# Causal attention with 16 heads of width 8: value products for eight heads at a time, two heads to 32 array columns, and a new layout of all jobs of a batch

## The chip, the cores and the metric

One core of one Trainium2 chip runs the kernel. The metric is the device time of one execution in microseconds (us); lower is better.

## The reference, cut to what matters

```python
xn = layernorm(x)                               # x: (8, 512, 128) f32
q, k, v = split(xn @ w_attn.T + b_attn)         # 16 heads of width 8
att = (q @ k.T) / sqrt(8), causal
S  = relu(att of head 0), column 0 and the diagonal set to 0
FF = cumsum over the queries of S shifted down by one row
att = att - FF                                  # for every head
keep = the 101 smallest FF of a row (fewer in the first rows), and the diagonal
y = softmax(where(keep, att, -inf)) @ v
attn = y @ w_proj.T + b_proj
# router: top 2 of 8 experts per token
ffn = sum over e of gate_e * (relu(xn @ wi.T + bi + (xn @ A_e.T) @ B_e.T) @ wo.T + bo)
out = x + attn + ffn
```

## The kernel before, in words

Eight batches are worked through one after the other. A batch's attention is cut into 44 units: for a tile `a` of 128 queries (four of them) a unit is four heads (`a` = 0), two heads (`a` = 1) or one head (`a` = 2, 3), against the `a + 1` key tiles up to the diagonal (`UNITS`, L59). Units are numbered through over all batches, and every engine runs the same loop over steps `t`, from -26 to the end, each in its own program and held together by semaphores. In step `t`

- PE makes the scores of unit `t` (`score`, L895) into one of three banks `ps_s`, turns unit `t - 4` by transposes into one of two banks `ps_t` (`turn`, L914), fills the jobs that the plan puts into this step (`fill`, L749), and, where unit `t - 5` ends a group of four heads, makes the value products of the group (`weigh`, L927): one f32 product for every head and key tile, which the trace shows as two instructions. The stationary operand is 32 columns of `va` (8 of v, one of ones for the sum of the weights, and what comes next), the moving one 128 columns of the exponentials `pr`. Four heads stand beside one another in the 128 array columns, and write 32 partitions each of `ps_o`.
- DVE adds the mask and takes the maximum of each row (L1320, L1327 for tile 0, L1330 for the others); POOL subtracts it (L549, `ar`); ACT takes the exponential out of `ps_t` into one of six buffers `pr` (L734). ACT waits with it until the products that read the buffer before are done.

When all groups of a query tile are done, ACT copies `ps_o` to `out_t` (L743, `taken`); the next tile's first group waits for that. The job `ot` (L869) turns the copy back by four transposes, DVE divides by the sums (L1292, L1294), the job `yt` (L875) transposes the result, ACT copies it, and the job `proj` projects three tiles (`proj0`) and then the last (`proj1`), with DVE adding the rest and SP storing `res` (L368).

A job is a piece of PE work with a step, one of two banks `ps_m` and a reader (ACT or DVE). `class Plan` (L134) sorts the jobs by step; a job waits for the read of the one that had its bank before, two jobs ago. The steps are written out by hand: `FFN_JOBS`, `OT_AT`, `YT_AT`, `PROJ_AT` count from a batch's own first unit, `PREP_AT` counts from the first unit of the batch before, since a batch is prepared while the one before it is worked on; `FIRST_AT` and `SECOND_AT` do so for the first two. Preparing is: layernorm (`moments`, `root`, `norm`, `xt`), q and k, each cut into three bf16 parts (`rest`, `second`, `third`), their head-stacks `qs`, `ks`, v (`v0`, `v1`: one copy each of v for two key tiles, one of the router's logits), head 0's scores (`s0` to `s3`, L812, read by ACT, L696), the sums over the queries (`forget`, L1085, `scan0` to `scan3`), their transposes (`f0` to `f3`), a search for the cut that keeps 101 keys (`search`, `under`, `reach`, `marks`, `top`, `replace`), a check (`flag`) and the masks (`mask_0` to `mask_3`, POOL, L536). The feed-forward part has `z`, two router masks (`mask0`, `mask1`), eight `h` jobs and two `down` jobs; ACT reads the `h`, POOL adds two of them to `hsum` (L563).

SP issues all transfers in one order (L432): the stacks of the next batch (`make_stacks`, 12 transfers of 128 KB), the second store of the batch before, the fetch of an input, the first store of this batch, and `make_first_heads` for the batch after the next (L400: 12 transfers of 8 KB, six for q and six for k). `s0` waits for these (`topped`, L820).

## Time and profile before

| | |
|---|---|
| median of 3 runs | 660.26 us (660.19 to 662.8) |
| the profiled execution | 663.88 us, its span 661.9 us |
| busy over the span | PE 561.8, DVE 505.3, POOL 445.7, ACT 378.0 us |
| mean granted TensorE clock | 0.958 |

Times are us unless marked ns. PEld is PE's weight load, which overlaps its products. "Idle before", in brackets at the end of a timeline row, is how long the engine had nothing to do before it, and what ended that. A busy PE is not a PE at its peak, since each instruction is shown with the tail in which the next one already runs: the step from one start to the next tells what it costs. Where a row says "x32", 32 instructions of a line are merged.

### The profile page before, as it was taken

How to read it: one execution, taken by the hardware profiler on the slowest of the kernel's cores; microseconds unless marked ns; L12 is line 12 of the kernel's file. 1: busy time of each engine (PE TensorE's matmuls, PEld its weight loads, DVE VectorE, ACT ScalarE, POOL GpSimd, SP SyncE). 2: the span in 40 equal slices, each digit the busy share in tenths (PEclk: the TensorE clock that was granted, in tenths of full speed). 3: DMA queues.
4: the chain of work that ended last, by engine and by line, in shares of the span. 5: the costliest groups of instructions: out<-in, count | busy, mean ns of one | idle time of the engine just before them, and what ended most of it. 6: DMA issues, size and time to landing. Idle time of an engine off the chain costs nothing.

```text
span 661.9 us, 16486 instructions
## 1 busy us (share of the span) xinstructions
PE 561.8 (85%) x5434; PEld 382.5 (58%) x5434; DVE 505.3 (76%) x1832; ACT 378.0 (57%) x815; POOL 445.7 (67%) x756
## 2 busy tenths in 40 slices
PE   4636879989888899889998898989998899899994
PEld 1413555766466665656566565666566565776583
DVE  7679798667997679857897769867897769975351
ACT  3452776565765565754756566664756556455542
POOL 7506948696578746796478955798478956496451
PEclk9656999999999899989999999999999999999998
DMA  4152052134001520025100430025000430000000
GB/s 100 25 63 27 1 63 35 30 47 61 1 17 28 65 30 1 18 47 63 11 18 17 60 45 1 17 43 70 9 1 18 60 44 1 2 14 5 1 2 17
DMA packets 30068, 19.56 MB, mean 30 GB/s; under 512 B 6089, under 2 KB 29856, under 8 KB 29984
## 3 DMA queue, kind: packets, MB, share of 16 engines
q1 hardware_dynamic: 29984, 18.50, 19.5%
q8 instruction: 45, 0.74, 0.5%
q14 instruction: 39, 0.32, 0.2%
HBM read 3.22 MB, written 2.10 MB: 8 GB/s over the span
## 4 chain that ended last, share of the span: by engine, by line
PE 41%; DVE 19%; POOL 15%; issue 11%; ACT 7%; SPq 4%; DMA 1%; DVEq 1%; ACTq 0%; POOLq 0%
PE ps_t L923 10%; POOL ar L549 9%; PE ps_o L942 9%; PE ps_s L910 6%; PE ps_m L855 4%; SPq L407 4%; DVE ar L1330 4%; ACT work L648 2%; PE ps_m L851 2%; DVE work L1150 2%; PE ps_m L867 2%; ACT pr L734 2%; POOL hsum L563 1%; PE ps_m L873 1%; PE ps_m L885 1%
## 5 line engine op out<-in xcount | busy, mean ns | idle before, releaser
L549 POOL TENSOR_SCALAR ar<-ar,mx 128x512 f32<-128x512 f32 (+3 forms) x512 | 280.2, 561 | 171.4 <-DVE mx L1330 165.1
L734 ACT ACTIVATE pr<-ps_t 128x512 f32<-128x512 f32 (+1 forms) x352 | 192.4, 558 | 80.9 <-PE ps_t L923 78.8
L1330 DVE CUSTOM_DVE_ANT_0 ar<-ps_s,mask 128x256 f32<-128x256 f32 (+2 forms) x384 | 202.9, 550 | 33.2 <-PE ps_s L910 32.3
L923 PE MATMUL ps_t<-ident,ar 128*128 128x128 f32 x1280 | 202.6, 277 | 16.5 <-POOL ar L549 11.0
L923 PEld LDWEIGHTS ps_t<-ident,ar 128*128 128x128 f32 x1280 | 156.2, 142 | 57.2 <-POOL ar L549 27.4
L910 PE MATMUL ps_s<-ks,qs 96*128 96x512 bf16 (+3 forms) x512 | 130.4, 307 | 11.7 <-DVE mx L1327 6.0
L942 PE MATMUL ps_o<-pr,va 128*32 128x128 f32 x2560 | 98.8, 282 | 7.6 <-ACT pr L734 6.1
L942 PEld LDWEIGHTS ps_o<-pr,va 128*32 128x32 f32 x2560 | 63.4, 111 | 48.5 <-ACT pr L734 31.2
L910 PEld LDWEIGHTS ps_s<-ks,qs 96*128 96x128 bf16 x512 | 43.1, 99 | 56.5 <-issue 27.1
L719 ACT ACTIVATE h<-ps_m,bi_col 128x512 f32<-128x512 f32 x64 | 43.9, 687 | 54.9 <-PE ps_m L855 54.2
L855 PE MATMUL ps_m<-zm,b_t 128*128 128x512 f32 x128 | 67.7, 610 | 8.7 <-ACT h L719 8.7
L563 POOL TENSOR_TENSOR hsum<-h 128x512 f32<-128x512 f32 x32 | 42.5, 1329 | 0.0
L648 ACT ACTIVATE work<-nf,cut 128x384 f32<-128x384 f32 (+1 forms) x48 | 31.7, 666 | 15.5 <-DVE cut L1128 10.8
L855 PEld LDWEIGHTS ps_m<-zm,b_t 128*128 128x128 f32 x128 | 21.7, 189 | 30.1 <-issue 15.3
L1091 DVE TENSOR_TENSOR_SCAN ft<-ones,s 128x511 f32<-128x511 f32 (+3 forms) x32 | 30.4, 959 | 6.2 <-POOL s L520 5.7
L851 PE MATMUL ps_m<-xnt,wi_t 128*128 128x512 f32 x64 | 33.5, 605 | 1.2 <-ACT h L719 1.2
L696 ACT ACTIVATE s<-ps_m,not_first 128x128 f32<-128x128 f32 (+3 forms) x29 | 15.2, 522 | 31.7 <-PE ps_m L821 27.3
L1189 DVE MAX8 top<-work 128x8 f32<-128x400 f32 (+3 forms) x64 | 30.9, 504 | 1.9
L1330 DVE DVE_READ_ACCUMULATOR2_ANT mx<- 128x1 f32 x384 | 31.4, 82 | 0.0
L1197 DVE MATCH_REPLACE8 work<-top,work 128x400 f32<-128x400 f32 (+3 forms) x64 | 31.3, 492 | 0.0
L867 PE MATMUL ps_m<-wo_t,hsum 128*128 128x128 f32 x256 | 31.2, 275 | 0.0
L867 PEld LDWEIGHTS ps_m<-wo_t,hsum 128*128 128x128 f32 x256 | 29.8, 192 | 0.1
(227 smaller groups left out, 772.1 us busy)
## 6 DMA issues: line engine op xcount, KB each, us to landing
qs<-parts SPq DMA_DIRECT2D x42, 128.0 KB
ks<-parts SPq DMA_DIRECT2D x42, 128.0 KB
xs<-in_L_attn_x SPq DMA_DIRECT2D x8, 256.0 KB, 3.0
out<-res SPq DMA_DIRECT2D x8, 192.0 KB, 2.0
first_heads<-parts SPq DMA_DIRECT2D x72, 8.0 KB
qs<-parts SPq DMA_DIRECT2D x12, 64.0 KB
ks<-parts SPq DMA_DIRECT2D x12, 64.0 KB
out<-res SPq DMA_DIRECT2D x8, 64.0 KB, 10.5
```

Source lines behind the costliest of these rows:

```text
L549: nc.gpsimd.tensor_scalar(col, col, -1.0, mx[:, t % NA_RING, j:j + 1], ALU.mult, ALU.add)\
L563: nc.gpsimd.tensor_tensor(hsum[:, f, :], h[:, 2 * (f % 2), :], h[:, 2 * (f % 2) + 1, :], ALU.add).then_inc(h_sum, 1)
L648: nc.scalar.activation(work[:, a, PADS:PADS + P * (a + 1)], nf[:, OFF[a]:OFF[a + 1]], ACT.Sign, bias=cut[:, a:a + 1], scale=-float(2 ** (R ...
L719: nc.scalar.activation(h[:, 2 * (f % 2) + j, :], m[:, :], ACT.Relu, bias=bi_col[:, f:f + 1])\
L734: nc.scalar.activation(pr[:, u % NP_RING, 0:w], ps_t[u % NT_RING][:, 0:w], ACT.Exp, scale=-1.0)\
L851: nc.tensor.matmul(m[:, :], wi_t[:, P * f:P * f + P], xnt[:, n % 2, :], start=True, stop=False)
L855: last = nc.tensor.matmul(m[:, :], b_t[:, P * f:P * f + P], zm[:, j, :], start=False, stop=True, skip_group_check=(j == 1))
L867: last = nc.tensor.matmul(m[:, P * a:P * a + P], hsum[:, f, P * a:P * a + P], wo_t[:, f, :], start=False, stop=(a == hi - 1 and f == NF - 1))
L910: last = nc.tensor.matmul(ps_s[u % NS_RING][:, w * j:w * j + w], qs[:, k % 2, h0 + j, P * a:P * a + P], ks[:, k % 2, h0 + j, 0:w], start=T ...
L923: last = nc.tensor.transpose(ps_t[u % NT_RING][:, P * j:P * j + P], ar[:, u % NA_RING, P * j:P * j + P], ident[:, :])
L942: last = nc.tensor.matmul(ps_o[OW * j:OW * j + OW, P * group:P * group + P], va[:, k % 2, c, VW * hh:VW * hh + OW], pr[:, (NU * k + unit) ...
L1330: nc.vector.tensor_tensor_reduce(out=ar[:, t % NA_RING, w * j:w * j + w], in0=ps_s[t % NS_RING][:, w * j:w * j + w], in1=mask[:, k % 2, OF ...
```

## The change

- `weigh` runs for eight heads (`OCT`): head pairs share 32 array columns. `va` holds a pair in 41 columns: 9 of the one head, 9 zeros from column 16, 9 of the other head from column 32. The stationary window of 32 columns starts at column 0 for the one head and at 16 for the other, so that each adds zeros to the other's 9 partitions, and both are summed into the same 32 partitions. `ORDER` names the heads so that the eight come out in order.
- A query tile takes 256 columns of `ps_o`, and two tiles share the bank: `taken`, `ot` and `yt` run twice in a batch, and the projections take two tiles each.
- `pr` has 11 buffers. Room for them comes from buffers that others lie in now: `s0` in `work`, `ft` in `hsum`, `qk32` in `h`, `ones` is a quarter as wide. New waits keep them apart.
- v is copied in four pieces per job. `first_heads` takes six transfers with q and k in one, and SP makes them ahead of the first store.
- The steps of all jobs are set anew.

```diff
-OW = 512 // NH
+OW = 32
+HALF_OW = OW // 2
+PAIR = 41
+OUT_COLS = HALF_OW * NH
...
-NA_RING, NP_RING = 7, 6
+NA_RING, NP_RING = 7, 11
...
-QUAD = 4
-GROUPS = NH // QUAD
-GROUP_OF = [GROUPS * a + h // QUAD for a, h, g in UNITS]
+QUAD, OCT = 4, 8
+GROUPS = NH // OCT
+GROUP_OF = [GROUPS * a + h // OCT for a, h, g in UNITS]
+
+ORDER = [8 * (i // 8) + 2 * (i % 4) + i % 8 // 4 for i in range(NH)]
...
-FIRST_FFN = ffn_jobs(6, (17, 19), (22, 24, 27, 30), (34, 36))
-FFN_JOBS = ffn_jobs(4, (8, 8), (15, 18, 21, 23), (29, 31))
-OT_AT, YT_AT, PROJ_AT = (12, 19, 36, 50), (17, 22, 39, 52), (40, 55)
-ATT_JOBS = [(f"ot{a}", OT_AT[a], "dve") for a in range(NA)] + [(f"yt{a}", YT_AT[a], "act") for a in range(NA)] + \
+FIRST_FFN = ffn_jobs(3, (17, 18), (19, 22, 24, 26), (40, 42))
+FFN_JOBS = ffn_jobs(4, (6, 10), (16, 18, 22, 24), (29, 30))
+OT_AT, YT_AT, PROJ_AT = (20, 52), (21, 53), (45, 54)
+ATT_JOBS = [(f"ot{a}", OT_AT[a], "dve") for a in range(2)] + [(f"yt{a}", YT_AT[a], "act") for a in range(2)] + \
...
-    "flag": 24, "mask_0": 24, "mask_1": 24, "v0": 21, "v1": 26, "marks_middle": 26, "top0_middle": 26,
-    "replace0_middle": 27, "top1_middle": 27, "replace1_middle": 28, "marks_wide": 25, "top0_wide": 25,
-    "replace0_wide": 26, "top1_wide": 26, "replace1_wide": 27, "last": 29, "mask_2": 30, "mask_3": 32,
-    "route": 30, "choices": 37, "share": 38,
+    "flag": 24, "mask_0": 24, "mask_1": 24, "v0": 10, "v1": 17, "marks_middle": 26, "top0_middle": 26,
+    "replace0_middle": 27, "top1_middle": 29, "replace1_middle": 30, "marks_wide": 25, "top0_wide": 25,
+    "replace0_wide": 26, "top1_wide": 28, "replace1_wide": 29, "last": 31, "mask_2": 32, "mask_3": 32,
+    "route": 26, "choices": 38, "share": 39,
...
-    "moments": -23, "root": -23, "norm": -5, "xt": -4, "q": 9, "k": 10, "rest_q": 10, "second_q": 11,
-    "third_q": 12, "rest_k": 11, "second_k": 12, "third_k": 12,
+    "moments": -23, "root": -23, "norm": -5, "xt": -4, "q": 9, "k": 12, "rest_q": 10, "second_q": 11,
+    "third_q": 12, "rest_k": 13, "second_k": 14, "third_k": 15,
...
-    "moments": -22, "root": -17, "norm": -15, "xt": -12, "q": -11, "k": -10, "rest_q": -10, "second_q": -9,
-    "third_q": -8, "rest_k": -9, "second_k": -8, "third_k": -7, "v0": 11, "v1": 13, "route": 14, "choices": 22,
-    "share": 23, "s0": 3, "s1": 5, "s2": 7, "s3": 9, "scan0": 6, "scan1": 6, "scan2": 10, "scan3": 12, "f0": 9,
-    "f1": 12, "f2": 13, "f3": 15, "search": 16, "under": 22, "reach": 23, "marks_narrow": 24,
-    "marks_middle": 26, "marks_wide": 27, "top0_narrow": 24, "top0_middle": 26, "top0_wide": 29,
-    "replace0_narrow": 27, "replace0_middle": 28, "replace0_wide": 30, "top1_narrow": 34, "top1_middle": 31,
-    "top1_wide": 35, "replace1_narrow": 35, "replace1_middle": 31, "replace1_wide": 35, "flag": 37,
-    "mask_0": 38, "mask_1": 38, "mask_2": 41, "mask_3": 45,
+    "moments": -30, "root": -17, "norm": -15, "xt": -12, "q": -11, "k": -10, "rest_q": -10, "second_q": -9,
+    "third_q": -8, "rest_k": -9, "second_k": -8, "third_k": -7, "v0": 15, "v1": 15, "route": 15, "choices": 21,
+    "share": 31, "s0": 3, "s1": 5, "s2": 7, "s3": 9, "scan0": 6, "scan1": 9, "scan2": 10, "scan3": 12,
+    "f0": 11, "f1": 11, "f2": 14, "f3": 14, "search": 15, "under": 21, "reach": 23, "marks_narrow": 28,
+    "marks_middle": 24, "marks_wide": 26, "top0_narrow": 28, "top0_middle": 25, "top0_wide": 27,
+    "replace0_narrow": 28, "replace0_middle": 26, "replace0_wide": 29, "top1_narrow": 31, "top1_middle": 36,
+    "top1_wide": 29, "replace1_narrow": 35, "replace1_middle": 36, "replace1_wide": 37, "flag": 38,
+    "mask_0": 40, "mask_1": 40, "mask_2": 44, "mask_3": 47,
 }
 PREP_JOBS = [("xt", "act"), ("q", "act"), ("k", "act"), ("v0", "act"), ("v1", "act")] + \
...
-        bias_rows = sb("bias_rows", [ROWS, 2, NA - 1, C], BF16)
+        bias_rows = sb("bias_rows", [ROWS, 2, 2, C], BF16)
...
-        va = sb("va", [P, 2, NA, (NH - 1) * VW + OW])
-        s0 = sb("s0", [P, FOFF[NA]])
-        ft = sb("ft", [P, FOFF[NA]])
+        va = sb("va", [P, 2, NA, NH // 2 * PAIR + VW])
         nf = sb("nf", [P, OFF[NA]])
         work = sb("work", [P, NA, WIDE])
+
+        s0_place = ((0, 1), (1, 1), (2, 1), (1, 3 * P + 2))
+
+        def s0(j, lo, hi):
+            row, at = s0_place[j]
+            return work[:, row, at + lo:at + hi]
...
+        qk32 = h
...
+        ft = hsum[:, :, :].rearrange("p f t -> p (f t)")
...
                         wait_full(sp, "s3", m - 1)
-                        for t in range(2):
-                            sp.wait_ge(split, 2 * m + t + 1)
-                            part = (Q_PART, K_PART)[t]
-                            for j in range(len(part)):
-                                sp.dma_start(first_heads[8 * j:8 * j + 8, t, :], parts[0:P:NH, t, part[j], :])\
-                                    .then_inc(topped, 16)
+                        sp.wait_ge(split, 2 * m + 2)
+                        for j in range(len(Q_PART)):
+                            lo, hi = Q_PART[j], 3 + K_PART[j]
+                            sp.dma_start(first_heads[8 * j:8 * j + 8, :, :],
+                                         parts[0:P:NH, :, :, :].rearrange("p t j c -> p (t j) c")[:, lo:hi + 1:hi - lo, :])\
+                                .then_inc(topped, 16)
...
                             fetch(k + 3)
-                        store(sp, k, 0)
                         if k + 2 < B:
                             make_first_heads(k + 2)
+                        store(sp, k, 0)
...
+                    link(nc.gpsimd.memset(work[:, 0:3, 0:1], 0.0))
+                    link(nc.gpsimd.memset(work[:, 1, 3 * P + 1:3 * P + 2], 0.0))
                     link(nc.gpsimd.memset(va[:, :, :, :], 1.0))
+                    for p in range(NH // 2):
+                        link(nc.gpsimd.memset(va[:, :, :, PAIR * p + HALF_OW:PAIR * p + HALF_OW + VW], 0.0))
...
                                     if f == 0:
+                                        if k + 1 < B:
+                                            wait_full(pool, f"f{NA - 1}", k + 1)
...
+                                    if n >= 2:
+                                        act.wait_ge(h_sum, NF * (n - 1))
...
-                                    act.wait_ge(scanned, NA * (n - 1) + j + 1)
+                                    act.wait_ge(mask_done, NA * (n - 1) + s0_place[j][0] + 1)
...
-                                copy(va[:, into(n), both, 0:NH * VW].rearrange("p a (h d) -> p a h d", d=VW)[:, :, :, 0:HD],
-                                     m3[:, :, 0:P].rearrange("p a (h d) -> p a h d", d=HD), name, n, False)
+                                for i, a in enumerate(half):
+                                    for s in range(2):
+                                        copy(va[:, into(n), a, 0:NH // 2 * PAIR]
+                                             .rearrange("p (h d) -> p h d", d=PAIR)[:, :, OW * s:OW * s + HD],
+                                             m3[:, i, 0:P].rearrange("p (h s d) -> p h s d", s=2, d=HD)[:, :, s, :],
+                                             name, n, False)
...
                                 f, j = int(name[1]), int(name[2])
+                                act.wait_ge(rested, 2 * min(n + 2, B))
...
-                            for a in range(NA):
+                            for a in (1, 3):
                                 if t == NU * kk + LAST[a] + LAG_P + OUT_LAG:
...
-                            last = nc.tensor.transpose(m[:, 0:P], y[:, a, :, :].rearrange("p h d -> p (h d)"), ident[:, :])
+                            for i in range(2):
+                                last = nc.tensor.transpose(m[:, P * i:P * i + P],
+                                                           y[:, 2 * a + i, :, :].rearrange("p h d -> p (h d)"), ident[:, :])
...
-                        if group == 0 and NA * k + a >= 1:
-                            pe.wait_ge(taken, NA * k + a)
-                        elif group == 0:
+                        if group == 0 and a % 2 == 0 and 2 * k + a // 2 >= 1:
+                            pe.wait_ge(taken, 2 * k + a // 2)
+                        elif group == 0 and a == 0:
...
+                        col = OUT_COLS * (a % 2) + P * group
                         for c in range(a + 1):
-                            for j in range(QUAD):
-                                hh = QUAD * group + j
+                            for j in range(OCT):
+                                hh = OCT * group + j
+                                quarter, odd = j % QUAD, j // QUAD
                                 unit, at = PLACE_OF[a, hh]
                                 at = P * (at + c)
-                                last = nc.tensor.matmul(ps_o[OW * j:OW * j + OW, P * group:P * group + P],
-                                                        va[:, k % 2, c, VW * hh:VW * hh + OW],
+                                from_v = PAIR * (ORDER[hh] // 2) + HALF_OW * odd
+                                last = nc.tensor.matmul(ps_o[OW * quarter:OW * quarter + OW, col:col + P],
+                                                        va[:, k % 2, c, from_v:from_v + OW],
                                                         pr[:, (NU * k + unit) % NP_RING, at:at + P],
-                                                        start=(c == 0), stop=(c == a))
+                                                        start=(c == 0 and odd == 0), stop=(c == a and odd == 1))
...
-                            link(nc.vector.memset(ft[:, FOFF[a]:FOFF[a] + 1], 0.0))
...
-                        for a in range(1, NA - 1):
+                        for a in range(1, 2):
                             link(nc.vector.tensor_copy(bias_part[:, :, :, a, :], bias_part[:, :, :, 0, :]))
...
-                        if j == 0 and n >= 1:
-                            wait_full(dve, f"f{NA - 1}", n - 1)
+                        if j == 0 and n == 1:
+                            wait_full(dve, f"f{NA - 1}", 0)
+                            dve.wait_ge(w_rows, 32)
+                        elif j == 0 and n >= 2:
+                            wait_full(dve, "down1", n - 2)
...
-                                    y[:, a, :, :], o3[:, :, 0:HD],
-                                    rec[:, :].rearrange("p (h o) -> p h o", o=1).to_broadcast([P, NH, HD]), ALU.mult)\
+                                    y[:, 2 * a:2 * a + 2, :, :].rearrange("p a h d -> p (a h) d"), o4[:, :, 0:HD],
+                                    rec[:, :].rearrange("p (g o) -> p g o", o=1).to_broadcast([P, 2 * NH, HD]), ALU.mult)\
```

## Rows read from the trace of the kernel before

**Rows 1.** the chain that ended last: shares by engine, by line

```profile
PE 41%; DVE 19%; POOL 15%; issue 11%; ACT 7%; SPq 4%; DMA 1%; DVEq 1%; ACTq 0%; POOLq 0%
PE ps_t L923 10%; POOL ar L549 9%; PE ps_o L942 9%; PE ps_s L910 6%; PE ps_m L855 4%; SPq L407 4%; DVE ar L1330 4%; ACT work L648 2%; PE ps_m L851 2%; DVE work L1150 2%; PE ps_m L867 2%; ACT pr L734 2%; POOL hsum L563 1%; PE ps_m L873 1%; PE ps_m L885 1%
```

**Rows 2.** windows by batch: length, then PE, PEld, DVE, ACT, POOL, clock

```profile
65.00:140.60 75.60, 64.90 (x620) 43.82 (x620) 61.93 (x224) 48.29 (x104) 56.39 (x88) 0.99 0.22 31
140.60:215.40 74.80, 66.54 (x675) 45.94 (x674) 60.78 (x227) 45.96 (x101) 55.38 (x93) 1.00 0.21 32
215.40:292.50 77.10, 68.34 (x675) 47.42 (x674) 61.61 (x225) 46.14 (x101) 53.33 (x93) 0.97 0.22 30
292.50:367.00 74.50, 67.03 (x668) 45.66 (x668) 59.06 (x221) 45.12 (x98) 52.44 (x90) 0.98 0.22 29
367.00:441.00 74.00, 66.62 (x674) 45.80 (x672) 60.10 (x224) 45.94 (x99) 53.92 (x91) 1.00 0.21 31
441.00:517.00 76.00, 67.56 (x682) 46.87 (x683) 62.32 (x228) 46.57 (x101) 56.51 (x98) 1.00 0.20 29
...
590.00:662.00 72.00, 61.23 (x660) 42.48 (x658) 31.87 (x117) 33.04 (x63) 36.82 (x62) 0.97 0.02 6
```

**Rows 3.** timeline of PE, two product calls and a job: start, length

```profile
370.59 0.43 PE L942 MATMUL ps_o<-pr,va 128*32 128x128 f32 x8
370.95 0.39 PE L910 MATMUL ps_s<-ks,qs 96*128 96x256 bf16 x2
...
426.04 0.60 PE L873 MATMUL ps_m<-ident,out_t 128*128 128x128 f32 x4
426.57 1.08 PE L942 MATMUL ps_o<-pr,va 128*32 128x128 f32 x32
427.58 0.39 PE L910 MATMUL ps_s<-ks,qs 96*128 96x512 bf16 x1
```

**Rows 4.** copies on ACT by line: count, ns shortest/median/longest, starts, forms

```profile
L743 ACT ACTIVATE out_t<-ps_o x32: 591/599/607, 70.0 to 653.2; 128x512 f32<-128x512 f32 x32
...
L575 ACT ACTIVATE yt<-ps_m x32: 255/274/289, 87.5 to 655.7; 128x128 f32<-128x128 f32 x32
L575 ACT ACTIVATE va<-ps_m x15: 363/387/392, 50.2 to 534.9; 128x256 f32<-128x256 f32 x15
L575 ACT ACTIVATE no_bias<-ps_m x15: 172/177/178, 50.5 to 535.2; 128x16 f32<-128x16 f32 x15
```

**Rows 5.** timeline of SP; then PE's waits: total, times, longest

```profile
433.13 7.31 SPq L407 DMA_DIRECT2D first_heads<-parts  x12
440.54 3.92 SPq L397 DMA_DIRECT2D qs<-parts  x6
...
PE ps_m L821 <- DMA first_heads<-parts: 10.4, 6, 2.1
...
PE ps_m L821 <- DVE zm L1277: 5.4, 6, 1.2
```

**Rows 6.** timeline of PE, longest wait for first_heads; a window behind it

```profile
291.21 0.38 PE L821 MATMUL ps_m<-first_heads 96*128 96x512 bf16 x1 [2.10 <-DMA first_heads<-parts]
...
294.10 1.64 PE L942 MATMUL ps_o<-pr,va 128*32 128x128 f32 x32
...
292.00:294.00 2.00, 2.00 (x5) 0.59 (x3) 0.62 (x4) 0.80 (x2) 2.00 (x5) 0.50 0.58 79
```

**Rows 7.** timeline of DVE, two scores, last batch; its waits for scores

```profile
641.02 0.69 DVE L1330 CUSTOM_DVE_ANT_0 ar<-ps_s,mask 128x512 f32<-128x512 f32 x1
...
641.67 0.69 DVE L1330 CUSTOM_DVE_ANT_0 ar<-ps_s,mask 128x512 f32<-128x512 f32 x1
...
DVE ar L1330 <- PE ps_s L910: 32.3, 37, 3.5
```

**Rows 8.** timeline of POOL at the start

```profile
4.52 1.22 POOL L477 MEMSET va<- 128x1336 f32 x1
...
18.89 0.23 POOL L493 TENSOR_SCALAR minus_mean<-mv 128x4 f32<-128x4 f32 x1 [3.55 <-DVE mv L1016]
```

More of the change, by code:

```diff
@@ L194, in build @@
         ident16 = sb("ident16", [P, P], BF16)
-        ones = sb("ones", [P, T])
+        ones = sb("ones", [P, P])
         causal = sb("causal", [P, P])
@@ L722, in _ @@
                                 a = int(name[2])
-                                if n >= 1 and a in (0, 3):
-                                    wait_full(act, ("proj0", "proj1")[a == 3], n - 1)
-                                copy(yt[:, a, :], m[:, 0:P], name, n)
+                                if n >= 1:
+                                    wait_full(act, f"proj{a}", n - 1)
+                                copy(yt[:, 2 * a:2 * a + 2, :].rearrange("p a t -> p (a t)"), m[:, 0:2 * P], name, n)
                         u = t - LAG_T
@@ L870, in fill @@
                             a = int(name[2])
-                            pe.wait_ge(taken, NA * n + a + 1)
-                            for c in range(GROUPS):
+                            pe.wait_ge(taken, 2 * n + a + 1)
+                            for c in range(4):
                                 last = nc.tensor.transpose(m[:, P * c:P * c + P], out_t[:, P * c:P * c + P],
```

51 lines of the change are left out of this document (25 added, 26 removed).

## The prediction

> **What bounds the kernel now.** The chain that ended last comes first: TensorE (PE) holds 41% of it, VectorE (DVE) 19%, GpSimd (POOL) 15%, the SP queue 4%, waits that the profile can't name 11% [rows 1]. No engine holds it alone: by line the turning of the scores, POOL's shift and the value products stand close together. The stretches from one batch's router product to the next come second [rows 2]: six inner batches take 74.0 to 77.1 us, with PE busy for 65 to 68 of them, DVE for 59 to 62, POOL for 52 to 57, ScalarE (ACT) for 45 to 48. The last batch, with DVE busy for 31.87 us only, still takes 72 us. The reader is to see there that taking half of DVE's work away saved hardly 3%: PE's queue, with its waits, sets the pace through most of a batch, and the others set it only at the edges. Third is PE's own order of time inside a batch [rows 3], for the price of one call, and fourth the waits ahead of PE [rows 5].
>
> **Value products.** Work stays: per batch 320 product instructions before and after, with the same 128 columns. What goes is calls, 16 per batch before, 8 after. From the start of a call to the start of the next score is 0.36 us for 8 instructions and 1.01 for 32 [rows 3]: 27 ns each and about 0.14 us per call. Ahead of the call comes another gap. The four transposes show 0.60 us there, 0.16 of it the last one's tail as the call's own 1.08 us has one, and 0.53 lie between their start and the call's, so some 0.09. I take 0.24 us a call with both. 64 calls fewer give 15.4 us of PE time. How much of it is path? The line has 9% of the chain, 60 us [rows 1], of 2560 x 27 ns plus 128 x 0.24 us, 100 us: 0.6. Taken: **-9.2 us**. Bounds: 0 and -15.4.
>
> **Output tiles.** Two query tiles of 256 columns fill the bank that one filled, so 32 copies of it on ACT become 16, and 32 jobs of four transposes become 16. A job costs PE 0.53 us with its gap [rows 3]; 16 x 0.53 is 8.5 us. Its line has 1% of the chain, 6.6 us of 17, so 0.39. Taken: **-3.3 us**, bounds 0 and -8.5. ACT loses 16 x 0.60 us of copies and 16 of 32 small yt copies, which become wider ones [rows 4]; that is off the path, since ACT is busy 45 to 48 us of a batch. If that cover goes, it is a gain of some 10 us more on ACT alone. DVE has 16 reciprocals and 16 products fewer, of twice the width; I cost them at nothing, under the same waits.
>
> **The v copies.** One copy of 0.387 us per v job becomes four of a quarter of the width. The rows bound one of 128x64 between 0.177 us (128x16) and 0.274 us (128x128) [rows 4], nearer to the lower end in columns: 0.21. So ACT gets 4 x 0.21 - 0.39, 0.45 us more per job, and both v jobs now lie in one step (15, before 11 and 13). With the two bias-free copies that is a block of 2.0 us on ACT (1.8 to 2.5), and queued behind it are the exponentials that the next turn needs for its bank. Two banks give PE one step of some 1 us. Taken: 0.4 us a batch, **+3 us**, bounds 0 and +10.
>
> **The first heads.** PE waited six times for these transfers, 10.4 us, 2.10 at most [rows 5, 6]. SP issues 12 of them behind the store of the first projection, in 7.31 us [rows 5]. Now 6 wider ones stand ahead of the store, whose own wait (proj0, step 40, now 45) no longer holds them. What they wait for instead is the third part of k at step 37, just before. An issue costs 0.61 us in this row, next to the 0.65 us of one with 128 KB in the row under it; twice the bytes should not double it. So 3.7 to 3.9 us of issue in place of 7.31 (7.3 at the worst), and a start up to a few us earlier: the longest wait, 2.10, is covered. Behind them in SP's queue the store and then the next batch's 12 stack transfers move later; the stacks aren't needed for a whole batch, and the store's buffer not before the next proj0. Stretches that ended with such a wait on the chain took 75.6, 74.8, 77.1 and 76.0 us, the other two 74.5 and 74.0 [rows 2]: 1.6 us apart, four times. Taken: **-6.5 us**, bounds -1 and -10.4 plus what the clock gives (below).
> After the 2.10 us wait PE's granted clock is 0.50, its lower level of 1.2 GHz, in the next 2 us and a product call of 32 takes 1.64 us [rows 6], against 1.08 [rows 3]. Part of the 1.6 us is this. The Trainium skill, "TensorE: Matmul & The Clock Gate", the section on the HAM clock gate, says that the throttled state is the default and that activity releases it. By that rule a shorter gap gives more than its own length, and by the same rule a new gap costs more than its own.
>
> **Router masks.** Both mask products lay in step 8 and their readers on DVE ran back to back; PE waited 5.4 us for them at the s job alone [rows 5]. Now they are in steps 6 and 10, with one scan moved from 6 to 9. Taken: **-3 us**, bounds 0 and -5.4.
>
> **Aliases.** The head-0 scores, the forgetting sums and q, k lie in buffers of other steps now. Each brings a wait: s on masks of 7 steps before, the first sum of h on f3 (14, against 17), the sums on down1, far back, q on the sums of h (25, against 33). All have slack of two steps or more, so nothing. A late f3 would be paid by POOL's sum and then by ACT's h.
>
> **The rest.** At the start, POOL fills a va of twice the size (+1.22 us) and ten small pieces more, about 3 us in all; a little later it sits idle for 3.55 us [rows 8], and DVE saves 1 to 2 us of small sets and copies. Taken 0, bounds -2 and +3. At the end, the last call has 64 instructions instead of 32 (+0.88 us) and six operations on two tiles; twice the width costs 0.11 us (0.274 to 0.387 [rows 4]), so +0.7; the call four steps before, 1.0 us [rows 3], is gone, and I count half of it. Taken **+1.1 us**.
>
> Sum: -9.2 - 3.3 + 3 - 6.5 - 3 + 0 + 1.1 = -17.9 us. Against the profiled execution's 663.9 us (span 661.9) that is 646.0; it ran 3.6 us over the median, so against 660.26 it is 642.4. **Forecast 642 us**, itself 634 to 652 for the spread of the terms.
>
> **Rivals.**
> *PE's work comes off in full* (chance 0.12). For it speaks the last batch, 72 us with DVE at 31.87. Then -15.4 - 8.5 - 10.4 - 3 + 2 is -35: 625 us.
> *PE is not what the time hangs on.* (0.19) DVE's and POOL's chain takes over, 59 to 62 and 52 to 57 us busy in a batch [rows 2] and in step with each other, and PE's freed time turns into waits for them. Only the transfers and half of the tiles' work come off, and the v block costs its 3: -6.5 - 1.6 + 3 + 1.1, about -4 to -8: 654 us. The inner 74.0 us stretch, which has no late transfer, speaks for it.
> *Long calls starve the scores* (0.12), the case on the other side. A call of 64 instructions holds PE for 32 x 27 ns more than one of 32: 1.9 us, plus the next score's 0.22. DVE eats one 512-column score in 0.65 us (two follow at that distance [rows 7]), and there are three score banks, so 1.95 us of supply. From a supply below 2.1 us on, and always where a long job of the feed-forward part lies beside it, DVE and behind it POOL run dry. Each batch has two such calls in each of tiles 1, 2 and 3, 0.43, 0.65 and 0.86 us longer: 3.9 us a batch, 31 in all. If half shows, 15.5, and the call's gain of 9.2 is lost, 642 becomes 667 us. Against it: DVE and POOL have 12 to 20 us of slack in a batch to catch up.
> *The new layout opens a gap in PE at each batch and the clock falls there* (0.07). Two us at 0.50 lose 1.0 us and the call behind them 0.56 [rows 6], with a gap of 2 us itself 3.6; seven times is 25, so 667 us. This is the rule named above from the Trainium skill, "TensorE: Matmul & The Clock Gate", used against the change. Against it: idle time moves from PE only where PE was the later one.
> *The change doesn't do what it says*: the product count is plain in the code, so no chance of its own.
>
> **Numbers.** The forecast's case has 0.50, and with the rivals' 0.12, 0.19, 0.12 and 0.07 that is all. The least that a measurement of this kernel can tell from no change is about 0.5%, 3.3 us, so faster is below 657 us. Faster: 0.48 of the forecast's case, the full one, and 0.14 of the second, 0.74. Within it: 0.02 of the first, 0.05 of the second and 0.01 of the starved one, 0.08. Slower: 0.11 of the starved and the clock's 0.07, 0.18. The range takes in the full case's centre and the second rival and stops at the mild end of the slower ones, 625 to 663 us, which leaves out some 0.15 above and 0.05 below.
>
> **What would show it.** Right: 64 product calls and 16 output jobs; PE busy per inner batch down by 2 to 3 us with the stretch down by about as much (72 us); no wait for first_heads, SP's six issues under 6 us; granted clock 1.00 in the stretches that show 0.97 now. Wrong: DVE idle for the scores after long calls, up from 32.3 us in all [rows 7]; ACT's block at step 15 followed by a PE wait for pr; batches still at 74 us with the same PE gaps for POOL; or new waits of PE over 2 us with the clock at 0.50 behind them.

## The result, and the profile after

The changed kernel takes **632.10 us** (median of four, 630.34 to 633.98), the kernel before beside it 660.23 (658.28 to 662.8). The ratio is 0.9573, with a 95% interval from 0.9527 to 0.9618: faster by 4.3%. The profiled execution took 633.0 us with a span of 631.2, so it is 0.9 over its median, where that of before was 3.6 over. The forecast was 642; 632.1 lies in its range (625 to 663), 2 us below the forecast case's own (634 to 652).

The profile's page of the changed kernel, busy time, then the chain that ended last by engine and by line (lines moved: L549 of before is L566, L910 L938, L923 L951, L942 L973, L1330 L1362):

```profile
PE 538.6 (85%) x5370; PEld 377.6 (60%) x5370; DVE 500.2 (79%) x1795; ACT 371.1 (59%) x831; POOL 447.5 (71%) x766
...
PE 35%; DVE 24%; POOL 23%; issue 9%; ACT 6%; SPq 1%; DVEq 0%; DMA 0%; ACTq 0%; POOLq 0%
POOL ar L566 14%; PE ps_t L951 8%; PE ps_m L881 7%; DVE ar L1362 6%; PE ps_o L973 6%; PE ps_s L938 4%; POOL mask L553 4%; PE ps_m L877 3%; DVE work L1229 3%; POOL zm L525 2%; DVE top L1221 2%; ACT work L667 2%; POOL parts L530 2%; ACT pr L760 1%; ACT h L745 1%
```

PE fell from 41% of the chain to 35, the SP queue from 4 to 1, the products' line from 9 to 6; POOL rose from 15% to 23 [rows 1]. The time came off PE and off a transfer, and the chain of DVE and POOL now holds more of what is left.

The same, windows by batch, each from the first score of a batch that DVE reads to the next batch's (columns as in [rows 2]):

```profile
133.45:204.12 70.67, 64.10 (x660) 45.47 (x659) 60.11 (x222) 44.16 (x101) 53.00 (x91) 0.98 0.24 38
204.12:274.04 69.92, 63.46 (x668) 45.45 (x667) 60.75 (x221) 45.28 (x102) 54.32 (x93) 1.00 0.24 33
...
416.76:486.55 69.79, 63.41 (x668) 45.39 (x667) 60.65 (x220) 45.12 (x102) 54.25 (x93) 1.00 0.23 29
...
554.28:631.20 76.92, 63.35 (x724) 46.13 (x722) 36.56 (x121) 35.63 (x66) 43.64 (x77) 0.97 0.03 9
```

The kernel before, cut at the same point, in a batch with the full clock:

```profile
436.43:510.65 74.22, 66.53 (x676) 45.93 (x675) 60.64 (x225) 45.95 (x100) 54.82 (x93) 1.00 0.20 28
```

An inner batch went from 74.2 us to 69.8: 4.4 off, of which PE's busy time is 3.1 and its waits the rest, while DVE and POOL have the same work. By this cut the batches of before take 83.2, 74.2, 76.9, 76.2, 74.9, 74.2, 74.2 and 77.1 us, those of after 82.0, 70.7, 69.9, 72.8, 69.9, 69.8, 67.7 and 76.9. The first and the last gave 1.4 together. Of the second to the sixth batch of a kernel, those at full clock and without such a single wait as named below are alike within some 1 us, mostly within 0.1. They are called clean in what follows, and 74.2 and 69.8 us are clean ones. The 72.8 us batch holds one wait of 2.7 us for which the profile names nothing.

PE's timeline in the changed kernel: a call of eight heads, its neighbours, and the output job (start, length):

```profile
422.56 1.95 PE L973 MATMUL ps_o<-pr,va 128*32 128x128 f32 x64
424.45 0.39 PE L938 MATMUL ps_s<-ks,qs 96*128 96x256 bf16 x2
...
430.27 0.60 PE L899 MATMUL ps_m<-ident,out_t 128*128 128x128 f32 x4
430.80 0.65 PE L973 MATMUL ps_o<-pr,va 128*32 128x128 f32 x16
```

64 instructions take 1.89 us from start to start: 64 x 27 ns + 0.14, as read off [rows 3]. What DVE does meanwhile is in its timeline, with the waits for scores behind the two calls of 64 and the two of 48 in this batch (starts 422.56, 459.39, 471.65, 482.18):

```profile
424.88 0.42 DVE L1362 CUSTOM_DVE_ANT_0 ar<-ps_s,mask 128x256 f32<-128x256 f32 x1 [0.54 <-PE ps_s L938]
462.57 0.56 DVE L1362 CUSTOM_DVE_ANT_0 ar<-ps_s,mask 128x384 f32<-128x384 f32 x1 [0.20 <-PE ps_s L938]
475.05 0.69 DVE L1362 CUSTOM_DVE_ANT_0 ar<-ps_s,mask 128x512 f32<-128x512 f32 x1 [0.33 <-PE ps_s L938]
484.50 0.69 DVE L1362 CUSTOM_DVE_ANT_0 ar<-ps_s,mask 128x512 f32<-128x512 f32 x1 [0.59 <-PE ps_s L938]
```

DVE waits 0.2 to 0.6 us behind each of these calls; how much of that is due to their length, e4 tells. The waits, in all (total, times, longest), and SP's order of work around 413 to 430:

```profile
POOL ar L566 <- DVE mx L1362: 132.2, 121, 3.5
DVE ar L1362 <- PE ps_s L938: 39.7, 46, 4.0
PE ps_t L951 <- POOL ar L566: 16.5, 18, 1.4
PE ps_t L951 <- ACT pr L760: 8.2, 24, 0.8
PE ps_m L847 <- DMA first_heads<-parts: 2.5, 1, 2.5
```

```profile
413.30 3.96 SPq L419 DMA_DIRECT2D first_heads<-parts  x6
419.53 0.37 SPq L385 DMA_DIRECT2D out<-res  x1
420.00 3.88 SPq L410 DMA_DIRECT2D qs<-parts  x6
```

The first heads cost 3.96 us of issue instead of 7.31, and only one wait is left, in the first inner batch [rows 5]. DVE's waits for the scores rose from 32.3 [rows 7] to 39.7, but not in a clean batch, which has 2.5 us of them before and after. The rise lies in the first batch (1.6 us before, 7.9 after), in the first inner one behind the late first heads (2.6 and 5.5) and in the last (13.1 and 15.9).

### The profile page after: what moved, and what is told of

Its sections match the earlier page's. It is cut to its first block, busy times and chain, and to the rows that moved or that the text cites. A ratio compares the mean times of both kernels' runs of the same rounds, so it can differ in the third digit from the quotient of the medians.

```text
span 631.2 us, 16235 instructions
## 1 busy us (share of the span) xinstructions
PE 538.6 (85%) x5370; PEld 377.6 (60%) x5370; DVE 500.2 (79%) x1795; ACT 371.1 (59%) x831; POOL 447.5 (71%) x766
## 4 chain that ended last, share of the span: by engine, by line
PE 35%; DVE 24%; POOL 23%; issue 9%; ACT 6%; SPq 1%; DVEq 0%; DMA 0%; ACTq 0%; POOLq 0%
POOL ar L566 14%; PE ps_t L951 8%; PE ps_m L881 7%; DVE ar L1362 6%; PE ps_o L973 6%; PE ps_s L938 4%; POOL mask L553 4%; PE ps_m L877 3%; DVE work L1229 3%; POOL zm L525 2%; DVE top L1221 2%; ACT work L667 2%; POOL parts L530 2%; ACT pr L760 1%; ACT h L745 1%
## 5 line engine op out<-in xcount | busy, mean ns | idle before, releaser
L566 POOL TENSOR_SCALAR ar<-ar,mx 128x512 f32<-128x512 f32 (+3 forms) x512 | 285.1, 568 | 138.6 <-DVE mx L1362 132.2
L1362 DVE CUSTOM_DVE_ANT_0 ar<-ps_s,mask 128x256 f32<-128x256 f32 (+2 forms) x384 | 202.4, 549 | 46.8 <-PE ps_s L938 39.7
L951 PE MATMUL ps_t<-ident,ar 128*128 128x128 f32 x1280 | 203.3, 277 | 25.0 <-POOL ar L566 16.5
L951 PEld LDWEIGHTS ps_t<-ident,ar 128*128 128x128 f32 x1280 | 154.1, 143 | 78.7 <-POOL ar L566 38.4
L938 PE MATMUL ps_s<-ks,qs 96*128 96x512 bf16 (+3 forms) x512 | 130.4, 308 | 7.7 <-DVE mx L1359 5.4
L973 PE MATMUL ps_o<-pr,va 128*32 128x128 f32 x2560 | 84.0, 277 | 5.8 <-ACT pr L760 5.5
L973 PEld LDWEIGHTS ps_o<-pr,va 128*32 128x32 f32 x2560 | 66.4, 110 | 31.9 <-issue 17.6
L938 PEld LDWEIGHTS ps_s<-ks,qs 96*128 96x128 bf16 x512 | 44.4, 99 | 44.9 <-issue 22.7
L582 POOL TENSOR_TENSOR hsum<-h 128x512 f32<-128x512 f32 x32 | 40.6, 1268 | 0.0
L1123 DVE TENSOR_TENSOR_SCAN hsum<-ones,work 128x512 f32<-128x512 f32 (+3 forms) x32 | 31.3, 980 | 6.1 <-POOL work L537 6.1
L1221 DVE MAX8 top<-work 128x8 f32<-128x144 f32 (+3 forms) x64 | 31.1, 505 | 1.6
L1362 DVE DVE_READ_ACCUMULATOR2_ANT mx<- 128x1 f32 x384 | 31.1, 81 | 0.0
L553 POOL TENSOR_TENSOR mask<-nf,work 128x128 f32<-128x128 f32 (+3 forms) x32 | 27.7, 866 | 2.7
```

Source lines behind the costliest of these rows:

```text
L553: nc.gpsimd.tensor_tensor(mask[:, into(n), OFF[a]:OFF[a + 1]], nf[:, OFF[a]:OFF[a + 1]], work[:, a, PADS:PADS + P * (a + 1)], ALU.subtract)\
L566: nc.gpsimd.tensor_scalar(col, col, -1.0, mx[:, t % NA_RING, j:j + 1], ALU.mult, ALU.add)\
L938: last = nc.tensor.matmul(ps_s[u % NS_RING][:, w * j:w * j + w], qs[:, k % 2, ORDER[h0 + j], P * a:P * a + P], ks[:, k % 2, ORDER[h0 + j], ...
L951: last = nc.tensor.transpose(ps_t[u % NT_RING][:, P * j:P * j + P], ar[:, u % NA_RING, P * j:P * j + P], ident[:, :])
L973: last = nc.tensor.matmul(ps_o[OW * quarter:OW * quarter + OW, col:col + P], va[:, k % 2, c, from_v:from_v + OW], pr[:, (NU * k + unit) % ...
L1362: nc.vector.tensor_tensor_reduce(out=ar[:, t % NA_RING, w * j:w * j + w], in0=ps_s[t % NS_RING][:, w * j:w * j + w], in1=mask[:, k % 2, OF ...
```

## The experiments

Twelve kernels, each timed in five rounds beside the kernel before on the same chip, whose medians there were 660.29 (e1 to e4), 660.84 (e5 to e8) and 659.87 us (e9 to e12). "Steps" are the numbers of the plan. Differences between runs of a few us lie near what the intervals allow, so the length of a clean batch stands beside the medians where it bears on them.

**e1: the new steps in the kernel before**, and nothing else: `FFN_JOBS`, `FIRST_AT`, `SECOND_AT` and `PREP_AT` of the change.

```diff
-FFN_JOBS = ffn_jobs(4, (8, 8), (15, 18, 21, 23), (29, 31))
+FFN_JOBS = ffn_jobs(4, (6, 10), (16, 18, 22, 24), (29, 30))
...
-    "search": 16, ... "mask_0": 38, "mask_1": 38, "mask_2": 41, "mask_3": 45,
+    "search": 15, ... "mask_0": 40, "mask_1": 40, "mask_2": 44, "mask_3": 47,
```

> The kernel before with the changed kernel's steps for all preparing jobs and for the feed-forward jobs of batches 1 to 7; its four output jobs, its six buffers and its transfers stay. If fewer product calls and output jobs carry the gain (3.0 us of PE in a row per batch, 24 in all), the steps alone give 2 to 8 us: 652 to 658. If the new steps carry it, by ending PE's waits for masks and POOL, this kernel comes near the changed one: 636 to 645. If the steps only suit the new structure, it is at 660 or above.

Measured: 666.95 us, ratio 1.0094 (1.0057 to 1.0131). PE's waits in it:

```profile
PE ps_m L821 <- DMA first_heads<-parts: 21.1, 6, 4.5
...
PE ps_m L832 <- DVE res L1304: 7.5, 6, 1.3
```

The new steps alone lose, as the third case of the expectation had it. PE comes to the s job sooner, and the transfers, behind a store that waits for the projection at step 40, come no sooner: 21.1 us of wait in place of 10.4.

**e3: early first heads in the kernel before**: six wide transfers ahead of the store, old steps.

```diff
...
-                        store(sp, k, 0)
                         if k + 2 < B:
                             make_first_heads(k + 2)
+                        store(sp, k, 0)
...
```

> The kernel before with the first heads' transfers six instead of twelve and ahead of the first store, nothing else. The forecast's term: 6.5 us faster, 654, PE's wait for first_heads (10.4 us) near 0 and the granted clock at 1.00 in the inner batches. If POOL's masks hold the same place in the batch and only take over: under 2 us, 658 to 660, with the wait gone from PE and PE's waits for POOL longer by as much.

Measured: 667.79 us, ratio 1.0092 (1.0058 to 1.0127), slower where both cases expected a gain. PE's waits at the s jobs, then three batches by the windows:

```profile
PE ps_m L821 <- DVE zm L1277: 10.4, 6, 1.7
```

```profile
134.42:208.78 74.36, 66.80 (x676) 45.87 (x675) 60.60 (x225) 45.91 (x100) 54.55 (x93) 1.00 0.22 31
208.78:286.21 77.43, 69.70 (x676) 48.01 (x675) 60.84 (x225) 45.94 (x100) 54.54 (x93) 0.96 0.21 30
286.21:362.12 75.91, 68.34 (x676) 46.94 (x675) 60.66 (x224) 45.91 (x100) 54.55 (x93) 0.98 0.23 31
...
224.87:230.87 6.00, 5.69 (x37) 4.51 (x38) 3.98 (x20) 1.45 (x3) 4.12 (x10) 0.50 0.58 69
```

The wait for the transfer, at `s0`, is gone in full. The one for the second router mask, at `s3` some 10 us later, grew from 5.4 us [rows 5] to 10.4. So the s jobs wait 10.4 us in place of 15.8, and the kernel is slower all the same. The three batches are the same work, to the instruction. They differ in TensorE's clock behind the one wait of 1.73 us: at 1.00 throughout the batch takes 74.4 us, with some 3.4 us at 0.50 around and behind the wait 75.9, with some 6.8 us 77.4. So a microsecond at 0.50 costs a little under half of one, and a clean batch gained nothing from the early heads (74.4 against 74.2).

**e6: e3 and the router masks apart** (steps 6 and 10, `scan1` at 9).

> The third experiment (early first heads on the kernel before, 7.5 us slower than it) with the two router masks in steps 6 and 10 instead of 8 and 8 and the second scan in step 9. If the third experiment lost by PE's wait for the pair of mask products, with the granted clock at half behind it, tile 1 falls from 17.4 to 14.5 to 15.5 us a batch, the clock stays at 1.00, and the kernel takes 645 to 653. If POOL sets the pace there, with the masks of the next batch, it stays at 660 to 668.

Measured: 653.78 us, ratio 0.9885 (0.9859 to 0.9911): 14.0 below e3 and just over the 645 to 653 expected, with the clock at 1.00 in all six inner batches. A clean one:

```profile
281.95:355.10 73.15, 67.06 (x676) 45.89 (x675) 60.82 (x225) 45.73 (x100) 54.60 (x93) 1.00 0.23 32
```

The two waits stood one behind the other. The early heads alone gave nothing, and both together give 6.5 us: 1.1 in a clean batch, and most of the rest in batches in which the clock no longer falls. The masks apart without the early heads were not run.

**e5: e6 and the rest of the new steps**, which is e1 with the early heads.

> The first experiment (new steps on the kernel before) with the six first heads' transfers ahead of the store as well; product calls, output jobs and six buffers stay old. By stretches of a batch, the time between the first scores of its four query tiles, the first experiment had 8.2, 15.4, 28.5 and 23.2 us. If steps and transfers need each other, tile 0 falls to 4.2 to 4.7 as it did in the third experiment and the batch to 71.5, against 69.9 of the changed kernel: 638 to 645 us, and what is left to 632 is the structure. If the structure is what makes the new steps fit, 650 or more.

Measured: 646.23 us, ratio 0.9783 (0.9754 to 0.9813), a clean batch 72.1 us; it lies between the two ranges expected. The same steps that lost 6.7 us in e1 gain 7.6 here.

**e2: the old steps in the changed kernel**, the counterpart of e1.

> The changed kernel with the old steps of all preparing and feed-forward jobs; its two output jobs, calls for eight heads and first heads' transfers stay. If structure carries the gain: 634 to 641. If the steps carry it: 648 to 658. The difference to the changed kernel and the first experiment's to the kernel before are the same quantity if the two parts add up.

Measured: 676.92 us, ratio 1.0262 (1.0221 to 1.0303), 44.8 above the changed kernel and above both ranges, so the two parts do not add up.

```profile
PE ps_m L869 <- DVE y L1326: 15.9, 7, 2.5
```

Here the masks at step 8 meet the output job at 52, which is step 8 of the next batch; their bank waits for DVE's division, and the clock fell to 0.50 during or behind each of the six inner waits of 2.5 us. This collision of old steps with a new output job makes up 15.9 us of waits and what the clock lost by them; the rest of the 44.8 was not taken apart.

**e7: the late first heads in the changed kernel**: 12 transfers behind the store again.

> The changed kernel with the first heads' transfers again twelve and behind the store of the first projection, which waits for step 45 now. If the early transfers are a condition of the new layout: PE waits for first_heads for 4 us or more six times, tile 0 goes from 4.7 to 8 or 9 us, 652 to 662 in all. If POOL's masks hide the wait as in the kernel before: under 5 us slower, 632 to 637.

Measured: 682.15 us, ratio 1.0302 (1.0272 to 1.0331), 50.1 above the changed kernel; the first case, and 20 us over its range.

```profile
PE ps_m L847 <- DMA first_heads<-parts: 50.4, 6, 9.0
```

```profile
451.60 0.38 SPq L385 DMA_DIRECT2D out<-res  x1
452.07 7.31 SPq L420 DMA_DIRECT2D first_heads<-parts  x12
```

The store ahead of them waits for `proj0`, which the new plan has at 45. Early first heads are what makes that plan possible. Their place ahead of the store and their number, six for twelve (3.4 us less of issue), were not run apart.

**e8: the old selection steps in the changed kernel** (`search` to `mask_3`).

> The changed kernel with the old steps of the selection alone: search, under, reach, marks, top, replace, flag and the four masks; all else stays. If spreading DVE's selection over tiles 2 and 3 is what shortened tile 3 (25.5 to 22.2 us a batch), tile 3 goes back by 2 us or more: 645 to 655. If tile 3 was shortened by the jobs that left it (an output job and the first projection), this does nothing: 630 to 636.

Measured: 640.01 us, ratio 0.9676 (0.9651 to 0.9701), 7.9 above by the medians, between the two ranges expected, and 70.4 us in a clean batch against 69.8. PE's waits for ACT rose, at the turn from 8.2 to 18.4 us and at `h` from 6.5 to 13.6:

```profile
PE ps_t L951 <- ACT pr L760: 18.4, 36, 1.3
PE ps_m L881 <- ACT h L745: 13.6, 17, 1.4
```

**e4: calls of four heads in the changed kernel**: the order of the pairs, the accumulation over both heads of 32 columns and everything else stay, but each call is cut in two, so there are 128 again.

```diff
-                            for j in range(OCT):
+                            for quarter in range(QUAD):
...
-                        if 0 <= t - LAG_P < NU * B and ENDS_GROUP[(t - LAG_P) % NU]:
+                        if 0 <= t - LAG_P < NU * B and ENDS_FOUR[(t - LAG_P) % NU]:
```

> The changed kernel with its value products called after every four heads again, 16 calls a batch instead of 8; buffers, shared columns, two output jobs and all steps stay, so that 64 calls are added and nothing else. At 0.24 us a call all on the path: 15 us slower, 647. At the forecast's share of 0.6: 9 us, 641. If long calls starve DVE, shorter ones give something back: 632 to 636, with DVE's wait for scores down.

Measured: 633.75 us, ratio 0.9585 (0.9555 to 0.9614), 1.6 above the changed kernel and inside its interval. From its page (busy time, chain) and its waits:

```profile
PE 549.9 (87%) x5370; PEld 376.8 (60%) x5370; DVE 500.5 (79%) x1795; ACT 372.8 (59%) x831; POOL 447.3 (71%) x766
...
PE 53%; POOL 18%; DVE 12%; ACT 9%; issue 7%; DVEq 0%; ACTq 0%; POOLq 0%
```

```profile
DVE ar L1366 <- PE ps_s L939: 32.3, 37, 2.6
```

PE works 11.3 us more and the span is 1.0 longer. The clock has a part in both, as it fell in three inner batches here and in one of the changed kernel. A clean batch is free of that:

```profile
415.02:484.81 69.79, 64.38 (x668) 44.79 (x667) 60.60 (x220) 45.41 (x102) 54.33 (x93) 1.00 0.23 30
```

Beside the changed kernel's 69.8 us PE works 0.9 us more for its eight calls, waits 1.0 less, and the batch is as long. (The two other inner batches at full clock take 68.4 and 70.3 us, 0.9 less together than the changed kernel's 69.9 and 69.8.) The largest wait that went is one of 0.76 us for DVE's division, which the changed kernel has at the job `yt` in each clean batch; a short call between the jobs `ot` and `yt` fills it here. DVE waits 1.9 us for scores in this batch and 2.5 with long calls, so their length starves it by some 0.6 us. (Of the 7.4 us between the totals 32.3 and 39.7, 3.4 lie in the first inner batch, where PE waited 1.5 us for the first heads here and 2.5 in the changed kernel.) So PE's saving went into waits, some that it has anyway and some for engines that the long call feeds later. No run tells the two apart.

**e11: the price of an output job**: each of the 16 jobs does its four transposes twice, the same result over itself.

```diff
-                            for c in range(4):
+                            for c in (0, 1, 2, 3, 0, 1, 2, 3):
```

> The changed kernel in which each of the 16 output jobs does its four transposes twice, the same result over itself: about 0.44 us more on TensorE per job, 7 us in all, and nothing on other engines. This is the price on TensorE alone of the 16 jobs that the change took away. Theory A (TensorE's work counts in full): 639 us. Theory B (at the share of 0.39 of the prediction): 634.8. Theory C (absorbed by TensorE's waits, as the calls of four were): 632 to 633 us.

Measured: 636.76 us, ratio 0.9657 (0.9623 to 0.9691).

```profile
431.73 1.04 PE L899 MATMUL ps_m<-ident,out_t 128*128 128x128 f32 x8
432.69 0.65 PE L973 MATMUL ps_o<-pr,va 128*32 128x128 f32 x16
```

A job takes 0.96 us from start to start instead of 0.53 (the other one of each batch 0.87 instead of 0.44), 6.9 in all, and 4.7 of it show in the medians (5.5 by the ratios): a share of 0.7 to 0.8, between theories A and B. The two intervals overlap, but a clean batch agrees, with 70.4 us against 69.8.

**e10: the projections at 45 and 54** in e5's kernel (128 calls, 32 output jobs).

```diff
-OT_AT, YT_AT, PROJ_AT = (12, 19, 36, 50), (17, 22, 39, 52), (40, 55)
+OT_AT, YT_AT, PROJ_AT = (12, 19, 36, 50), (17, 22, 39, 52), (45, 54)
```

> The kernel before with the new steps and the early first heads (646.2 us), and with its two projections at steps 45 and 54 as well instead of 40 and 55; its 128 calls of products, 32 output jobs and six exponential buffers stay. It asks where the 14.1 us between 646.2 and 632.1 lie, of which calls of eight heads explain 1.6. Theory A (places): the projection at 40 collides with the masks that moved to 40, so 636 to 640 us, and the wait of the projection's product for DVE (4.2 us in all) goes. Theory B (number of jobs and copies): 645 to 647 us. Both ways the projection at 54 may cost at the end of the last batch, 0.5 us.

Measured: 642.28 us, ratio 0.9738 (0.9695 to 0.9782). By the medians 4.0 less than e5, though the intervals overlap; the profiles agree, with four inner batches of 71.1 us against 72.1 in e5, and PE's wait for `res` (4.2 us in e5) gone. (The profiled execution as a whole took 0.9 longer than e5's, by one batch of 78.3 us that holds a wait of 4.4 for which the profile names nothing.)

```profile
206.04:277.10 71.06, 65.61 (x678) 45.93 (x682) 59.46 (x225) 46.52 (x100) 54.64 (x93) 1.00 0.22 33
```

**e9: the v jobs at 11 and 13** in the changed kernel.

```diff
-    ... "v0": 15, "v1": 15, ...
+    ... "v0": 11, "v1": 13, ...
```

> The changed kernel with its two v jobs at steps 11 and 13 again, instead of both in step 15, where ScalarE has ten copies in a row. Theory A (the term of the prediction: the block costs 0.4 us a batch, 3 us in all): 629 us, and TensorE's wait for the exponentials (7.4 us in all in the changed kernel) down by 2 to 3 us. Theory B (the block is covered by the two turning banks): 632 us, within 1 us of the changed kernel. Theory C (15 was the free place and 11 and 13 now lie beside s and f jobs): slower, 634 to 640, with a wait of TensorE for ScalarE's v or s copies.

Measured: 639.86 us, ratio 0.9703 (0.9671 to 0.9736): 7.8 slower, where a gain of 3 had been one theory; theory C came out, and PE's wait for the exponentials at the turn stayed at 8.2 us.

```profile
PE ps_m L881 <- ACT h L745: 9.8, 23, 0.6
...
PE ps_m L858 <- ACT no_bias L594: 4.2, 8, 0.5
```

Steps 11 and 14 hold two f jobs each in the new plan, and the f job behind a v job now waits for its copies. What the block at step 15 costs is in ACT's timeline of the changed kernel:

```profile
440.75 0.58 ACT L594 ACTIVATE va<-ps_m 128x64 f32<-128x64 f32 x4 [1.37 <-PE ps_m L836]
441.18 0.22 ACT L594 ACTIVATE no_bias<-ps_m 128x16 f32<-128x16 f32 x1
441.24 0.62 ACT L594 ACTIVATE va<-ps_m 128x64 f32<-128x64 f32 x4
441.67 0.27 ACT L594 ACTIVATE no_bias<-ps_m 128x16 f32<-128x16 f32 x1
441.73 0.70 ACT L760 ACTIVATE pr<-ps_t 128x512 f32<-128x512 f32 x1
```

Ten copies in 0.98 us, since most of them start before the one ahead has ended; the exponential follows at once. In e9 a clean batch is 0.9 us longer (70.7); the first two lose 2.0 and 2.3, and how much of that is clock stays open.

**e12: the masks earlier** in the changed kernel.

```diff
-    "mask_0": 40, "mask_1": 40, "mask_2": 44, "mask_3": 47,
+    "mask_0": 39, "mask_1": 39, "mask_2": 42, "mask_3": 45,
```

> The changed kernel with GpSimd's masks at steps 39, 39, 42 and 45 instead of 40, 40, 44 and 47, so that less of them lies beside the batch's edge, where GpSimd works without a gap for some 17 us. Theory A (GpSimd bounds the edge, and work moved ahead of it comes off): 625 to 630 us, with the first two tiles of a batch about 1 us shorter. Theory B (the tile before has DVE and GpSimd at 88% and 83% already, and pays what the edge gains): 631 to 634 us. Theory C (the masks now wait for the selection's last step 38 and hold GpSimd's queue): slower, over 635 us, with a wait of GpSimd at the flag.

Measured: 628.66 us, ratio 0.9543 (0.9511 to 0.9576). First the changed kernel: the window around the edge of a batch that begins at 416.7, POOL's last mask in it, and PE's wait that follows in tile 1:

```profile
414.00:433.00 19.00, 16.47 (x219) 12.99 (x212) 14.72 (x44) 11.21 (x22) 18.67 (x41) 1.00 0.40 55
```

```profile
426.38 1.27 POOL L553 TENSOR_TENSOR mask<-nf,work 128x512 f32<-128x512 f32 x1
...
429.77 0.66 PE L951 MATMUL ps_t<-ident,ar 128*128 128x128 f32 x4 [1.44 <-POOL ar L566]
```

And the last mask in e12, whose batch begins at 416.1:

```profile
423.03 1.28 POOL L553 TENSOR_TENSOR mask<-nf,work 128x512 f32<-128x512 f32 x1
```

POOL works 18.67 of these 19 us. With the last mask 6.9 us into the batch instead of 9.7, the three clean batches of e12 take 69.0 to 69.1 us against 69.8 to 69.9, and the wait of 1.44 us, which five batches of the changed kernel have, is in none of them. That speaks for theory A, though tiles 0 and 1 became 0.4 us shorter together and not 1, and tile 2 another 0.4. The intervals of the two kernels overlap, and they were not timed side by side: that it beats the changed kernel by 3 us is likely, not shown.

## Why the prediction came out as it did

The sum was -17.9 us and the result -28.1, and the runs give a ladder from 660.3 to 632.1: early heads and masks apart 6.5 (e6; by medians from different chips, each beside 659.9 to 660.8 for the kernel before), the rest of the steps 7.6 (e5), the projections' places 4.0 (e10), and what is left 10.2. By the ratios, each beside the kernel before on its own chip, the same four are 7.6, 6.7, 3.0 and 10.9. A clean batch went from 74.2 us over 73.1, 72.1 and 71.1 to 69.8. What is left holds the pairs and their wider output tiles, and with them the eleven buffers, the v copies in four, the buffers that lie in others, and the steps of the output jobs and of the first batch's feed-forward part.

- **Product calls, -9.2 taken: the step that failed most.** The price of 0.24 us a call was somewhat high: e4's clean batch has 0.9 us more of PE's busy time for eight calls, so 0.12 a call, and all in all it has 11.3 us more for 64, a falling clock included, beside 15.4 worked out. The share of 0.6, read from the line's share of the chain, was wrong: 1.6 us show, and nothing in a clean batch. The rival of the starved scores names a real wait with a wrong size (some 0.6 us a batch by e4, 3.9 forecast and half of it taken); the rest of the saving fell into waits of PE, as the rival *PE is not what the time hangs on* had it.
- **Output tiles, -3.3 taken.** Undersized: at e11's share of 0.7, the 8.5 us of PE time are 5.9, if taking a job away gives what doubling it costs. With the calls' 1.6 that is 7.5 of the 10.2. The remaining 2.7 (the halved jobs of ACT and DVE, the banks' freer order, the eleven buffers and what else the last rung holds) were not taken apart. Of the buffers, a call for eight heads needs more than six from tile 2 on, where each head has its own; with six and short calls, before and in e10, the profile never names a product call as what ACT's exponential waited for.
- **First heads, -6.5, and router masks, -3.** Together they gave 6.5, and alone the first cost 7.5 us (e3). The step "stretches that ended with such a wait took 1.6 us more" took the wait for the cause. All six inner batches of before have one at `s0`, of 1.5 to 2.1 us, and with it the three at full clock still took 74.2, 74.9 and 74.2; the two of 76.9 and 76.2 are those that lost time to the clock. And behind the wait stood the router mask. The prediction's own question, what is late next, had its answer in the next row of the same group: the wait for zm of 5.4 us [rows 5].
- **v copies, +3: no cost was found.** A quarter copy lasts 0.25 us (0.21 estimated), but eight of them and two small ones took 0.98 us and not 2.0, because durations were added where starts count. And the old places were priced as if they were still free (e9: 7.8 us worse). One copy in place of four, in the new plan, was not run.
- **The steps of everything else: put at nothing.** Beyond the router masks and the v jobs the prediction has no term for the plan. The steps that e5 adds to e6 gave 7.6 and the projections' places 4.0, so 11.6 of the 28.1; in the new kernel the selection's steps alone are worth 7.9 (e8). This is the second step that failed, and the larger in size.
- **The end, +1.1.** From the last score's start on PE to the end of the span went from 15.2 us to 16.4: right.
- **What would show it.** 64 calls, 16 output jobs and an issue of 3.96 us came as said; PE's busy time fell by 3.1. The batch fell by 4.4, to 69.8 and not 72. One wait for the first heads is left, of 2.45 us with the clock at 0.50 behind it. DVE's longer waits for scores, named there as a sign against, came in the total, and not in the clean batches.

*PE's work comes off in full* (625 us) came nearer than the forecast, 7 us off and not 10, and not for its reason: e4 refutes it for the calls, while e11 bears it out for the output jobs to some three quarters. *PE is not the bound* (654) holds for the calls alone. *The new gap with a falling clock* is what e2, e3 and e7 are; the changed kernel has one such gap. That the time lies in the range is in part luck: the calls were put 7.6 too high, the first heads and masks 3.0, the v copies at a cost of 3 that did not show and the tiles 2.6 too low, and this met a gain of the plan of 11.6 that was in no term.

## What to carry to other kernels

A wait that is removed gives only what lies between it and the next one in the same stretch: read the next row of waits of that line before pricing the first. Compare batches of one kernel with one another before a longer one is put down to a wait: here it was the clock. A line's share of the chain is no price for making its calls fewer and longer; ask which waits of the engine stand beside the calls, and what the engines behind them do meanwhile. Steps, buffers and the order of a queue are to be tried together: the new steps alone were 7 us slower than no change (e1), the early heads alone 7.5 (e3), and the new kernel without either of them 17 (e2) and 22 (e7), 45 to 50 behind the whole.

## What the runs showed of the hardware

The length of a wait did not settle whether TensorE's clock fell behind it. Of PE's waits at the s jobs and the router mask in the inner batches, none of 1.51 to 1.58 us (four in the kernel before) was followed by 0.50; of those of 1.72 to 1.73 (e3) five in six were; of the two of 2.10 and 2.14 (before) one; of those of 2.45 to 4.5 (e1, e2 and one of the changed kernel) all thirteen; of those over 8 (e7) all six. But the wait of 2.7 us in the changed kernel for which the profile names nothing was not, though its like of 2.6 in e12 was, and in the kernel before a wait of 1.18 was, with others around it. In some of these the clock was down before the wait had ended. It stayed at 0.50 for 3 to 7 us (in e7 for up to 10, most of it during the wait), and e3's equal batches give its price without a model: 1.5 us for 3.4 us at 0.50, and 3.1 for 6.8.

The Trainium skill, "TensorE: Matmul & The Clock Gate", in Part 1 on the HAM clock gate, says that the chip derives this clock from how busy PE has been recently. The trace agrees in so far as the clock fell behind PE's waits in the cases counted here; that waits equal to 0.01 us are followed by nothing in one batch and by some 6.8 us at half the clock in another (e3) is what the prediction had no term for.
